# A recurrent layer on eight cores: two products per row go from VectorE to GpSimd, and half of the output stores change queue

## The reference

```python
xn = _layernorm(x)                         # x: (2, 4096, 2048)
prev = shift(xn); xx = prev - xn           # xk = xn + xx * tm_k, and so for v, r, g
r, k, v, g = xr @ Wr.T, xk @ Wk.T, xv @ Wv.T, sigmoid(xg @ Wg.T)
def step(carry, kv):                       # per channel, over time
    a, b = carry; kt, vt = kv
    ek = exp(kt); euek = exp(u) * ek
    out = (a + euek * vt) / (b + euek)
    return (w * a + ek * vt, w * b + ek), out
o = sigmoid(r) * wkv * g @ Wo.T
s = layernorm(o) * ln_g + ln_b
y = x + s * silu(xn @ ternary(weight).T + bias)
```

## Time and profile before

| | us |
|---|---|
| two timed runs, median (lowest to highest) | 1460.47 (1457.84 to 1463.10) |
| profiled execution, its own time | 1451.12 |
| profiled execution, span of its slowest core (core 3) | 1449.6 |
| spans of all cores | 1434.1 to 1449.6 |

### The profile page before, as it was taken

The page is one execution under the profiler, slowest core; times in us unless marked ns, Lnnn a source line. Parts: engine busy times, 40 slices in busy tenths (PEclk is TensorE's granted clock), DMA queues, the critical chain, the costliest instruction groups (busy, mean ns, idle before and its releaser), DMA issues. The chain is left out here.

```text
span 1449.6 us, 11807 instructions; the slowest of 8 cores (1434.1 to 1449.6 us)
## 1 busy us (share of the span) xinstructions
PE 827.1 (57%) x3834; PEld 362.8 (25%) x3834; DVE 524.6 (36%) x499; ACT 494.0 (34%) x660; POOL 100.7 (7%) x188
## 2 busy tenths in 40 slices
PE   2532220037949389999940876260687879885200
PEld 0110000013525145544420332130233334331000
DVE  0059998300010002767007056596210000000597
ACT  4632222112222121122212357457253343328221
POOL 0002222100000000011110000000000000000000
PEclk8555555568979699999985897695798989999555
DMA  3428888684261741655126433433524444300387
GB/s 116 147 91 276 263 255 265 172 258 147 79 201 43 255 149 68 183 171 168 40 81 230 132 121 99 134 122 118 169 83 121 121 126 119 121 15 0 98 248 234
DMA packets 79070, 211.65 MB, mean 146 GB/s; under 512 B 11424, under 2 KB 11424, under 8 KB 79008
## 3 DMA queue, kind: packets, MB, share of 16 engines
q1 hardware_dynamic: 55584, 143.76, 34.3%
q0 software_dynamic: 14208, 49.29, 9.2%
q10 hardware_dynamic: 9216, 17.83, 3.8%
HBM read 166.81 MB, written 39.85 MB: 143 GB/s over the span
## 5 line engine op out<-in xcount | busy, mean ns | idle before, releaser
L974 PE MATMUL rgo_ps<-mov_rg,rgo_wbf 128*128 128x512 bf16 x1024 | 237.1, 396 | 185.6 <-DMA mov_rg<-sxg 59.5
L405 PE MATMUL g1ps<-mov_kv,g1wbf 128*128 128x512 bf16 (+1 forms) x1536 | 262.4, 336 | 99.7 <-DMA mov_kv<-sxk 42.1
L821 ACT ACTIVATE rgo_wbf<-rgo_mw 128x512 bf16<-128x512 f32 x192 | 119.9, 633 | 271.7 <-DMA rgo_mw<-wg 92.5
L405 PEld LDWEIGHTS g1ps<-mov_kv,g1wbf 128*128 128x128 bf16 x1536 | 133.3, 101 | 228.7 <-issue 114.1
L974 PEld LDWEIGHTS rgo_ps<-mov_rg,rgo_wbf 128*128 128x128 bf16 x1024 | 103.2, 101 | 319.6 <-issue 209.3
L974 PE MATMUL rgo_ps<-wkv_sb,rgo_wbf 128*128 128x512 bf16 x512 | 117.9, 395 | 21.1 <-ACT sr_sb L950 11.7
L405 PE MATMUL g1ps<-xn_sb,g1wbf 128*128 128x512 bf16 x512 | 110.7, 379 | 0.0
L269 DVE CAST g1wbf<-g1mwstg 128x1024 bf16<-128x1024 f32 x24 | 16.7, 694 | 237.5 <-PE g1ps L405 98.3
L333 ACT ACTIVATE g1row<-g1ps 128x512 f16<-128x512 f32 (+1 forms) x96 | 44.8, 492 | 148.7 <-PE g1ps L405 138.6
L573 PE MATMUL ps_sc<-fs_a,ones 128*1 128x512 f16 x64 | 32.3, 610 | 84.5 <-ACT fs_a L618 84.5
L974 PEld LDWEIGHTS rgo_ps<-wkv_sb,rgo_wbf 128*128 128x128 bf16 x512 | 51.6, 101 | 87.4 <-issue 31.9
(11 more groups left out here) (112 smaller groups left out, 836.7 us busy)
## 6 DMA issues: line engine op xcount, KB each, us to landing
g1mwstg<-wf SPq DMA_DIRECT2D x64, 512.0 KB, 4.8
g1mwstg<-wk SPq DMA_DIRECT2D x32, 512.0 KB, 6.4
g1mwstg<-wv SPq DMA_DIRECT2D x32, 512.0 KB, 4.7
rgo_mw<-wr SPq DMA_DIRECT2D x64, 256.0 KB, 3.2
rgo_mw<-wg SPq DMA_DIRECT2D x64, 256.0 KB, 3.4
rgo_mw<-wo SPq DMA_DIRECT2D x64, 256.0 KB, 3.3
xstg<-x SPq DMA_DIRECT2D x16, 576.5 KB, 4.4
xst<-x SPq DMA_DIRECT2D x16, 512.0 KB, 4.6
```

Of the source, the lines that this page charges most:

```text
L405: mm = e.matmul(bank[:, :t1 - t0], wbf[hh % 2][:, ic, oc * 128:(oc + 1) * 128], s["mov"][:, ic, t0:t1], start=(ic == 0), stop=(ic == CH - 1))
L821: e.activation(wbf[ss % 2][:, ic, :], mwstg[jj % 2][:, :], AF.Copy).then_inc(sem["scs"], 1)
L974: mm = e.matmul(bank[:, :t1 - t0], wbf[ss % 2][:, ic, oc * 128:(oc + 1) * 128], phs[p]["mov"][:, ic, t0:t1], start=(ic == 0), stop=(ic == ...
```

## The change

The two first operations of each `chain` are taken out of VectorE's list and given to GpSimd. GpSimd's loop now has 18 turns; turn ci first makes the products of row ci - 2 (when ci is at least 2) and then issues the loads of row ci (when there is one). The factor cs is spread over a tile `cs_tile` of 128 columns by VectorE at the start, so that GpSimd multiplies two tensors. A semaphore `sgp` tells VectorE that a row's products are there. The loads of rows 2 and 3 no longer wait for chains 0 and 1.

In the closing stage all 16 stores of y are issued by GpSimd; SP has only the loads.

```diff
--- before.py
+++ after.py
@@ -57,7 +57,7 @@
 
     sem = {n: e0(nc.semaphore(n)) for n in
            ("sl", "sw0", "sw1", "scv", "scs", "smm", "sev", "st0", "st1",
-            "sv", "ss", "sden", "srd", "sg0", "sg1")}
+            "sv", "ss", "sden", "srd", "sgp", "sg1")}
     cnt = {n: 0 for n in sem}
 
     def snap():
@@ -743,6 +743,7 @@
                for i in range(NROW)]
         zar = ec(nc.sbuf_tensor("zar", [128, 1 + T_ALL], F32))
         zbr = ec(nc.sbuf_tensor("zbr", [128, 1 + T_ALL], F32))
+        cs_tile = ec(nc.sbuf_tensor("cs_tile", [128, LANE], F32))
         ps = [ec(nc.psum_tensor("rgo_ps%d" % i, [128, 512], F32))
               for i in range(8)]
         blk = es.enter_context(nc.Block())
@@ -841,32 +842,40 @@
 
         @blk.gpsimd
         def _(e):
-            for ci in range(CH):
-                if ci >= NROW:
-                    e.wait_ge(sem["sv"], b["sv"] + svord[("q", ci - NROW)])
-                elif ci >= 2:
-                    e.wait_ge(sem["sden"], b["sden"] + ci - 1)
-                stp = "st%d" % (ci % 2)
-                e.dma_start(ekr[ci % NROW][:, :],
-                            sek[ci, :, :]).then_inc(sem[stp], 16)
-                e.dma_start(vvr[ci % NROW][:, :],
-                            svd[ci, :, :]).then_inc(sem[stp], 16)
+            for ci in range(CH + 2):
+                if ci >= 2:
+                    cj = ci - 2
+                    m = cj % NROW
+                    e.wait_ge(sem["st%d" % (cj % 2)], st_row[cj])
+                    e.wait_ge(sem["ss"], b["ss"] + 1)
+                    e.tensor_tensor(ekr[m][:, 0:LANE], ekr[m][:, 0:LANE],
+                                    cs_tile[:, :], OP.mult)
+                    e.drain()
+                    inc(e.tensor_tensor(vvr[m][:, :], ekr[m][:, :],
+                                        vvr[m][:, :], OP.mult), "sgp")
+                if ci < CH:
+                    if ci >= NROW:
+                        e.wait_ge(sem["sv"],
+                                  b["sv"] + svord[("q", ci - NROW)])
+                    stp = "st%d" % (ci % 2)
+                    e.dma_start(ekr[ci % NROW][:, :],
+                                sek[ci, :, :]).then_inc(sem[stp], 16)
+                    e.dma_start(vvr[ci % NROW][:, :],
+                                svd[ci, :, :]).then_inc(sem[stp], 16)
 
         @blk.vector
         def _(e):
             e.memset(zar[:, 0:1], 0.0)
             e.memset(zbr[:, 0:1], 0.0)
+            e.memset(cs_tile[:, :], 1.0)
+            e.drain()
+            inc(e.tensor_scalar(cs_tile[:, :], cs_tile[:, :],
+                                cs_sb[:, 0:1], None, OP.mult), "ss")
             e.drain()
             for kind, l in v_events:
                 if kind == "chain":
                     m = l % NROW
-                    e.wait_ge(sem["st%d" % (l % 2)], st_row[l])
-                    e.drain()
-                    e.tensor_scalar(ekr[m][:, 0:LANE], ekr[m][:, 0:LANE],
-                                    cs_sb[:, 0:1], None, OP.mult)
-                    e.drain()
-                    e.tensor_tensor(vvr[m][:, :], ekr[m][:, :],
-                                    vvr[m][:, :], OP.mult)
+                    e.wait_ge(sem["sgp"], b["sgp"] + l + 1)
                     e.drain()
                     wbc = w_sb[:, l:l + 1].broadcast_to([128, T_ALL])
                     e.tensor_tensor_scan(zar[:, 1:], wbc, vvr[m][:, :],
@@ -1089,17 +1098,6 @@
                         "sw%d" % (ci % 2), 16)
                     inc(e.dma_start(g2ld[ci % 2][:, :], sg2[ci, :, :]),
                         "sw%d" % (ci % 2), 16)
-                    k = ci - 2
-                    if k >= 1 and k % 2 == 1:
-                        e.wait_ge(sem["sden"], b["sden"] + k + 1)
-                        inc(e.dma_start(y_d[k, :, :], outst[k % 2][:, :]),
-                            "sg0", 16)
-                for k in range(max(1, CH - 2), CH):
-                    if k % 2 == 1:
-                        e.wait_ge(sem["sden"], b["sden"] + k + 1)
-                        inc(e.dma_start(y_d[k, :, :], outst[k % 2][:, :]),
-                            "sg0", 16)
-                e.wait_ge(sem["sg0"], cnt["sg0"])
 
             @blk.scalar
             def _(e):
@@ -1122,7 +1120,7 @@
                 e.wait_ge(sem["ss"], b["ss"] + ci + 1)
                 e.wait_ge(sem[swp], b[swp] + 32 * (ci // 2 + 1))
                 if ci >= 2:
-                    stp = "st0" if ci % 2 == 0 else "sg0"
+                    stp = "st%d" % (ci % 2)
                     e.wait_ge(sem[stp], b[stp] + 16 * (ci // 2))
                 e.drain()
                 e.tensor_tensor(outst[ci % 2][:, :], sstg[ci % 2][:, :],
@@ -1149,11 +1147,12 @@
 
             @blk.gpsimd
             def _(e):
-                for ci in range(0, CH, 2):
+                for ci in range(CH):
                     e.wait_ge(sem["sden"], b["sden"] + ci + 1)
                     inc(e.dma_start(y_d[ci, :, :], outst[ci % 2][:, :]),
-                        "st0", 16)
+                        "st%d" % (ci % 2), 16)
                 e.wait_ge(sem["st0"], cnt["st0"])
+                e.wait_ge(sem["st1"], cnt["st1"])
 
     es_o.close()
     es0.close()
```

## The result

The changed kernel takes 1481.9 us (median of 11 runs, 1476.3 to 1535.0) against 1458.8 us (10 runs): the ratio is 1.0163, interval 1.0119 to 1.0206. By the ratio that is 24 us slower (the two medians lie 23.1 us apart), where no change was forecast and 1476 was the upper end. A few executions of either kernel were disturbed, which the ratio leaves out.

What follows compares the result with a forecast made beforehand. ScalarE's queue was taken to bound the scanning stage. Terms 0 + 0 + 0.7 turned 1451.1 into 1451.8 us (median 1460.5 into 1461.2); likeliest range 1450 to 1467, up to 1476 with other cases.

Steps and rivals of the forecast that it cites:

- What bounds the scanning stage: Between 748 and 1068 us, ScalarE's queue sets the pace; VectorE idles 14.45 us before a burst of reciprocals.
- The two multiplies leave VectorE: Scanning stage: 1.16 us less per row, 18.6 us for 16 rows, but worth nothing on the path.
- P: Time of GpSimd's two products per row in the scanning stage, taken as 3.0 us, upper end 4.8 us.
- Then come both products, P, and a handover: Scanning row after GpSimd's loads: products then 0.15 us handover, scans later by P - 0.26; step costs 0.
- the cover: Scanning stage: VectorE's slack before ScalarE waits, 3.74 us for the first burst's row, 14.45 us over four rows.
- three bursts by 4 x (P - 3.9): Scanning stage, if P exceeds 3.9 us: each burst late by this much, 11 us in all at P = 4.8.
- The loads of rows 2 and 3 and `cs_tile`: Loads start some microseconds earlier and the tile is made while VectorE waits; costed at 0.
- The stores: Closing stage: last store +1.1 us on GpSimd's queue, odd stores give back 0.4, so +0.7 us.
- GpSimd is slow enough to set the scanning stage: Rival, 0.15: slow products use up the slack; +11 us at P = 4.8, 1472; 2% slower needs P past 6.3.
- VectorE's relief counts: Rival, 0.05: the scanning stage follows VectorE, so 18.6 us come off, giving 1442.
- stores back up: Rival, 0.06: closing-stage stores run one after the other in one queue, about 15 us more, 1476.
- signs of being wrong: P over 3.9 us with ScalarE waiting, scanning stretch changed by over 5 us, or store waits in most closing rows.

Runs made afterwards that it cites:

- e8: The kernel before with ScalarE's reciprocals put in batches, 8 changes of function table and back instead of 16; measured 0.9879 of the kernel before.
- e6: The kernel before with one more scan per row on VectorE, into a tile nobody reads; measured 1.0029 of the kernel before.
- e7: The kernel before with two more scans per row on VectorE; measured 1.0067 of the kernel before.
- e1: The changed kernel with GpSimd's drain between its two products replaced by a semaphore wait; measured 1.0034 of the kernel before.
- e4: The kernel before with a probe on GpSimd's queue: drains behind no load or loads of different sizes; its own time says nothing.
- e5: The changed kernel with GpSimd's loop turned round, a row's products before the next row's loads, drain kept; measured 0.9973 of the kernel before.

## Why the prediction was wrong

**What bounds the scanning stage: right.** ScalarE's queue does: with fewer table loads in it the kernel gets shorter (e8). VectorE's work does not (e6 and e7), and VectorE can hold the stage back only through the wait for `sden`. That wait is the one that came.

**The two multiplies leave VectorE, worth nothing: right.** With the drain gone, e1 is not faster than before.

**P, the price of the products: right to a few per cent, and it was the wrong quantity.** I took 3.0 us, by the rate of the scan; the groups show 0.44 + 2.36 = 2.80 us for a row in GpSimd's timeline, 2.95 with the gap of e1. The estimate from the Trainium skill ("GPSIMD Engine Reference", § 3 Performance versus the Vector engine) was 2.8 us, and the rows agree in the sum; by the same 2.2 ns an element the two products would take 0.28 and 2.53 us, so two misses of opposite sign make the sum this close. The row of 13.13 us that the prediction gave is what e1 measured, to the hundredth by luck: P with its gap is 0.05 us shorter than I took, the way from `q` to the end of the loads 0.05 us longer (1.68 instead of 1.63).

**The step that failed** is "Then come both products, P, and a handover". The diff has an instruction between the products, a `drain`, and I gave it no term. I had counted VectorE's drains as gaps of under 0.1 us in the earlier trace rows and read GpSimd's as the same thing. On GpSimd it stands 0.44 us behind the issue of row 6's loads, which the same paragraph puts ahead of it, and waits for their landing: 2.5 to 4.9 us a row on the slowest core, from row 3 on. The term was to be had: the page before gave 3.2 and 3.8 us to landing for these loads.

With it the prediction's own thresholds give the loss. In the row shown, the scans start 906.73 - (898.86 + 0.69) = 7.18 us after `q` instead of 2.04, so they are 5.1 us late, where the cover was 3.7: 1.4 us over, and ScalarE waits 1.5 us there. The next four rows took 980.63 - 914.39 = 66.24 us instead of 4 x 10.39 = 41.56, 24.7 more, where the cover was 14.45: 10.2 us over, and ScalarE waits 9.66. Also mis-sized: "three bursts by 4 x (P - 3.9)". In the first burst only its last row can be late, since the chains before it were made in the long pause; so it lost 1.5 us and the next two 9.7 and 9.05.

**The loads of rows 2 and 3 and `cs_tile`: nothing seen of them.** The stretch before the first burst had 46.2 us of VectorE's idle time left.

**The stores: right in the main, the tail mis-sized.** VectorE's waits for stores remained as they were, 2.9 us in four rows against 3.2 in three; the stores don't back up. The end of the kernel (timeline of all engines, which answers to the earlier trace rows):

```profile
1483.37 1.23 DVE L1126 TENSOR_TENSOR outst<-sstg,g2ld 128x1024 f32<-128x1024 f32 x1 [1.90 <-DMA y<-outst]
1484.67 1.23 DVE L1129 TENSOR_TENSOR outst<-outst,xst 128x1024 f32<-128x1024 f32 x1
1486.45 0.53 POOL L1152 DMA_DIRECT2D y<-outst  x1 [3.90 <-DVE outst L1129]
```

The last store starts 0.55 us after the sum, as predicted, and lands in 2.9 us; the span ends 1.6 us later still, where SP's store left 0.3. So the tail is +2.1 us, not +1.1, and the 0.4 us that the odd stores should have given back don't show in the closing stage (+0.5 us).

**The rivals.** "GpSimd is slow enough to set the scanning stage" is the one that came, with its place, its wait and its threshold, but not by its cause: it needed slow products, and they are fast. I gave it 0.15. That VectorE's relief counts, and that stores back up, are both refuted. Of the signs of being wrong two came, ScalarE's wait for the chain and a stretch longer by over 5 us; P over 3.9 us, which was to be their cause, did not.

## What to carry to other kernels

When work moves to another engine, price every instruction that moves with it on the new queue, those that compute nothing too, and ask what is in flight there: on GpSimd a drain behind a load just issued cost that load's landing time here, and a semaphore on the one result that matters cost 0.14 us. Where the mover sits on a loop with a ring of buffers, work out how late a row may be before someone waits, and test it with a dose of idle work, as e6 and e7 do. And if one engine's queue sets a stage, shorten that queue: batching the reciprocals gained 1.2%, while relieving another engine gained nothing.

## What the runs showed of the hardware that was not expected

GpSimd's drain waits for the loads that GpSimd itself has in flight: 3.6 us behind 64 KB, 9.0 us behind four of 576 KB, 0.23 us behind none (e4; 2.83 the very first time). It does not wait for SP's loads: the drain of 0.23 us, over at 1225.85, passed while the weight slab that SP had issued at 1224.71 was still under way; it landed at 1228.81.

VectorE and GpSimd exclude each other in the rows of e5 in which both read two tensors in SBUF, rather than share. The product starts at 900.75 while L887 runs until 901.57, in its usual 1.28 us; 2.36 us of the product's own from then would end at 903.93, and it ended at 900.75 + 3.05 = 903.80. L891, under way since 901.49, ends at 904.88, 1.08 us after that, nearly its full 1.28. The Trainium skill says so in "SBUF — State Buffer", § Who interferes with whom: the read interface that both need is locked for a whole instruction. These rows agree.
